# A cross attention's scores and values moved to small tiles of the array

## What is computed

```
def _L2_xattn_ref(q, k, v):            # h = 8, d = dv = 16, Tq = Tk = 256
    qh, kh, vh = (z.reshape(B, h, d, T) for z in (q, k, v))
    qn = _l2norm(qh, axis=-2)
    kn = _l2norm(kh, axis=-2)
    qk = 5.0 * jnp.einsum('bhdq,bhdk->bhqk', qn, kn)
    sm = jax.nn.softmax(qk, axis=-1)
    out = jnp.einsum('bhqk,bhdk->bhdq', sm, vh)
    return out.reshape(B, Dv, Tq)
...
x = x + jnp.tanh(g_xattn[2]) * _L2_xattn_ref(_layernorm(x, axis=-1), ctx_2048, ctx_2048)
```

## Time and profile before

| | us |
|---|---|
| median of 3 runs | 1113.99 |
| lowest, highest | 1108.63, 1115.76 |
| span of the profiled execution | 1103.1 |
| TensorE, its loads busy | 982.7, 646.4 |
| VectorE, ScalarE, GpSimd busy | 703.1, 468.2, 354.8 |
| mean granted TensorE clock | 0.941 |

### The profile page before, as it was taken

The page is one execution under the profiler, slowest core; times in us unless marked ns, Lnnn a source line. Parts: engine busy times, 40 slices in busy tenths (PEclk is TensorE's granted clock), DMA queues, the critical chain, the costliest instruction groups (busy, mean ns, idle before and its releaser), DMA issues.

```text
span 1103.1 us, 18620 instructions
## 1 busy us (share of the span) xinstructions
PE 982.7 (89%) x6482; PEld 646.4 (59%) x6482; DVE 703.1 (64%) x1490; ACT 468.2 (42%) x779; POOL 354.8 (32%) x362
## 2 busy tenths in 40 slices
PE   7888989999977887877777989999989999989997
PEld 4466664435655444444453569998479575854443
DVE  5887754434798999999968781112411250289998
ACT  3343322100269999999953443332113436410000
POOL 4142130000464666666634112210410547410002
PEclk9898888999987999999988999997989999799999
DMA  9100020000000000000000051003631415100001
GB/s 274 25 1 1 1 88 4 1 0 1 1 1 1 2 1 0 0 0 0 0 27 1 1 167 36 1 1 114 149 115 49 141 46 159 52 1 0 0 0 38
DMA packets 54276, 41.30 MB, mean 37 GB/s; under 512 B 17569, under 2 KB 52028, under 8 KB 54220
## 3 DMA queue, kind: packets, MB, share of 16 engines
q1 hardware_dynamic: 52684, 36.36, 11.9%
q0 software_dynamic: 1536, 4.20, 1.2%
HBM read 33.20 MB, written 7.34 MB: 37 GB/s over the span
## 4 chain that ended last, share of the span: by engine, by line
PE 68%; DVE 16%; issue 9%; ACT 4%; DVEq 2%; DMA 1%; POOL 0%; SPq 0%; ACTq 0%; POOLq 0%
PE psum L442 6%; PE psum L949 6%; PE psum L1381 5%; PE psum L1402 5%; PE psum L940 5%; DVE xn L2007 3%; PE psum L479 3%; PE psum L1506 3%; PE psum L592 2%; PE psum L608 2%; PE psum L1220 2%; PE psum L422 2%; PE psum L955 2%; PE psum L446 2%; DVE am L1102 2%
## 5 line engine op out<-in xcount | busy, mean ns | idle before, releaser
L1040 POOL TENSOR_SCALAR arena<-arena 128x1024 f16<-128x1024 f32 x128 | 133.7, 1044 | 94.4 <-ACT arena L1014 91.4
L1102 DVE TENSOR_REDUCE am<-psum 128x1024 f32 (+1 forms) x128 | 155.0, 1212 | 8.7 <-PE psum L940 8.6
L1014 ACT ACTIVATE arena<-psum,am 128x1024 f32<-128x1024 f32 x128 | 143.0, 1125 | 10.3 <-DVE am L1102 8.1
L949 PEld LDWEIGHTS psum<-identh,arena 128*128 128x128 f16 x1024 | 63.1, 100 | 94.3 <-issue 61.2
L949 PE MATMUL psum<-identh,arena 128*128 128x128 f16 x1024 | 82.0, 225 | 37.2 <-DVE xn L1107 36.3
L1949 PE MATMUL psum<-arena,cT 128*128 x512 | 110.9, 379 | 3.3 <-DVE xn L2007 2.8
L316 POOL TENSOR_TENSOR rstd<-ve,neg_half 128x1 f32<-128x1 f32 x64 | 39.0, 613 | 207.6 <-DVE ve L306 207.3
L2007 DVE SCALAR_TENSOR_TENSOR xn<-psum,small,xn 128x256 f32<-128x256 f32 x248 | 102.2, 478 | 4.9 <-DVE xn L2007 2.2
L940 PE MATMUL psum<-arena 96*128 96x512 bf16 x256 | 78.8, 392 | 11.6 <-ACT arena L1014 8.8
L1949 PEld LDWEIGHTS psum<-arena,cT 128*128 128x128 f16 x512 | 49.9, 98 | 63.8 <-DVE xn L2007 4.0
L1007 ACT ACTIVATE arena<-psum,m 128x1024 bf16<-128x1024 f16 x64 | 71.7, 1121 | 2.4 <-PE psum L949 2.4
(11 more groups left out here) (338 smaller groups left out, 1876.5 us busy)
## 6 DMA issues: line engine op xcount, KB each, us to landing
hT<-in_L_ffn_expert_masks SPq DMA_DIRECT2D x32, 256.0 KB, 2.9
arena<-in_L_ffn_w_gate SPq DMA_DIRECT2D x2, 1408.0 KB
arena<-in_L_ffn_w_up SPq DMA_DIRECT2D x2, 1408.0 KB
arena<-in_L_ffn_w_down SPq DMA_DIRECT2D x2, 1408.0 KB
moe_in<-xT SPq DMA_DIRECT2D x2, 1024.0 KB, 6.9
hT<-moe_in SPq DMA_DIRECT2D x4, 512.0 KB, 6.2
moe_out<-arena SPq DMA_DIRECT2D x16, 128.0 KB, 1.7
weights<-in_L_ffn_w SPq DMA_DIRECT2D x2, 640.0 KB, 6.0
```

The source lines that it names most:

```text
L949: mm = pe.transpose(bank[:, k * P:(k + 1) * P], Y1[:, hm % 2, k * P:(k + 1) * P], identh)
L1014: act.activation(PE1[:, h % 2, :], scores, ACT.Exp, bias=am[:, bass.ds(n, 1)], accum_out=qs[:, bass.ds(n, 1)]).then_inc(sig("p1_ready"), 1)
L1040: pool.tensor_scalar(Y1[:, n % 2, :], PE1[:, n % 2, :], 255.0, 1024.0, ALU.mult, ALU.add)\
L1102: dve.tensor_reduce(am[:, bass.ds(n, 1)], psum[:, 2 * SCORES[h]:2 * SCORES[h] + 2, :], AX.XY, ALU.max, negate=True)\
```

## The change

Both kinds of matmul move to tiles of a part of the array.

- **Scores.** Four groups g of 32 partitions hold two heads each. `masked_keys` makes two copies of the keys instead of eight, by the parity of the head (`par`), 128x512 in one product, all eight batches in tiles of their own. A score matmul contracts over 32 rows: `keys[rows, k, 128 keys]` as weights, `xn[rows, b, :]` streamed, for g = 0 to 3 in turn, each group into its own bank. One unit u is one parity k of one batch, so 16 units of 8 score matmuls.
- **Exponentials.** ScalarE takes a pair of banks in one activation of 1024 columns. Three pairs of banks (0 to 5) go round; four slots of exponentials.
- **Values.** The weights are now the values: for each head 32 columns (`VP`), 16 of them zero, those of the other parity; the exponentials are streamed, 256 columns. Four groups write the four 32-partition parts of one bank's first half. Four more matmuls of the same kind with ones in place of values (`ones2`) write the sums to the other half. So 16 matmuls a unit, and the outputs come out with tokens on the partitions; the transposes go.
- **Additions.** VectorE takes the reciprocal of all 128x256 sums, multiplies output, gate and reciprocal, and adds to X. Banks 6 and 7 alternate by batch; TensorE waits on `o2_read` before it writes one again, and once more at the end of the stage and ahead of the shared expert.
- **GpSimd.** Clears `VP` and `ones2` and fills them in `values2_pool`, makes the first four batches' keys there, and the other four once the norms' squares are read, since they lie in `sq2`.

```diff
-        PT2 = a.tile([4, DC, 2, D])
+        PT2 = a.tile([4, 2, DC, D])
...
-        cA = a.tile([DC, NB, H2, D2 + 1])
-        KM = a.tile([2, H2, D])
+        VP = a.tile([DC, NB, H2, 2 * D2])
+        ones2 = a.tile([2, 2 * D2])
+        KM = a.tile([NB // 2, 2, D])
+        KM_late = sq2.rearrange("p (b k) d -> p b k d", k=2)
...
-        STEPS2 = NB * H2 // 2
-        LAG_V2, LAG_B2 = 2, 3
+        STEPS2 = NB * 2
+        PAIRS2, SLOTS2 = 3, 4
+        def pair_banks(p):
+            return 2 * (p % PAIRS2)
+        def out2_bank(b):
+            bank = psum[:, 6 + (b + ids["out2_first"]) % 2, :]
+            return bank[:, 0:D], bank[:, D:2 * D]
...
         def masked_keys(pool, b):
-            if b >= 2:
-                pool.wait_ge(ring_a.full, ids["s2", 4 * (b - 2) + 3])
-            pool.tensor_tensor(KM[:, b % 2, :, :], bc(cx[:, b, :].unsqueeze(1), [P, H2, D]),
-                               bc(mask8.unsqueeze(2), [P, H2, D]), ALU.mult).then_inc(sig("km_ready"), 1)
+            pool.tensor_tensor(keys_of_pair(b), bc(cx[:, b, :].unsqueeze(1), [P, 2, D]),
+                               bc(par.unsqueeze(2), [P, 2, D]), ALU.mult).then_inc(sig("km_ready"), 1)
...
+            pool.memset(ones2, 0.0).then_inc(sig("vp_ready"), 1)
+            pool.memset(VP, 0.0).then_inc(sig("vp_ready"), 1)
...
         def xa2_pe(pe):
             norms_pe(pe, "q2", sq2)
...
+            def scores(u):
+                b, k = divmod(u, 2)
+                if k == 0:
+                    pe.wait_ge(sig("km_ready"), b + 1)
+                    pe.wait_ge(sig("q2_ready"), b + 1)
+                if 2 * u + 1 >= PAIRS2:
+                    pe.wait_ge(sig("p2_ready"), 2 * u + 2 - PAIRS2)
+                for kc in range(DC):
+                    for g in range(4):
+                        rows = slice(32 * g, 32 * g + 32)
+                        bank = psum[:, pair_banks(2 * u + g // 2) + g % 2, :]
+                        mm = pe.matmul(bank[:, kc * D:(kc + 1) * D], keys_of_pair(b)[rows, k, kc * P:(kc + 1) * P],
+                                       xn[rows, b, :], start=True, stop=True)
+                        if kc == DC - 1:
+                            mm.then_inc(sig(f"s2_pair{g // 2}_full"), 1)
+            def values(u):
+                b, k = divmod(u, 2)
+                out, total = out2_bank(b)
+                if k == 0 and b >= 2:
+                    pe.wait_ge(sig("o2_read"), b - 1)
+                pe.wait_ge(sig("p2_ready"), 2 * u + 2)
+                for kc in range(DC):
+                    first, last = k == 0 and kc == 0, k == 1 and kc == DC - 1
+                    for g in range(4):
+                        p = PT2[:, (2 * u + g // 2) % SLOTS2, g % 2, kc, :]
+                        pe.matmul(out[32 * g:32 * g + 32, :], VP[:, kc, b, 2 * g + k, :], p,
+                                  start=first, stop=last, skip_group_check=True)
+                    for g in range(4):
+                        p = PT2[:, (2 * u + g // 2) % SLOTS2, g % 2, kc, :]
+                        mm = pe.matmul(total[32 * g:32 * g + 32, :], ones2[:, k, :], p,
+                                       start=False, stop=last, skip_group_check=True)
+                        if kc == DC - 1:
+                            mm.then_inc(sig("v2_done"), 1)
+            for u in range(STEPS2 + 1):
+                if u < STEPS2:
+                    scores(u)
+                if u >= 1:
+                    values(u - 1)
+            pe.wait_ge(sig("o2_read"), NB - 1)
...
+            for p in range(2 * STEPS2):
+                u = p // 2
+                act.wait_ge(sig(f"s2_pair{p % 2}_full"), 2 * (u + 1))
+                if u >= 2:
+                    act.wait_ge(sig("v2_done"), 4 * (u - 1))
+                at = pair_banks(p)
+                act.activation(PT2[:, p % SLOTS2, :, :, :].rearrange("p g c q -> p (g c q)"),
+                               psum[:, at:at + 2, :].rearrange("p g n -> p (g n)"), ACT.Exp, scale=ALPHA)\
+                   .then_inc(sig("p2_ready"), 1)
...
+                dve.wait_ge(sig("v2_done"), 8 * (b + 1))
+                step(dve.reciprocal(share, total))
+                step.wait()
+                dve.scalar_tensor_tensor(share, out, gate(4), share, ALU.mult, ALU.mult).then_inc(sig("o2_read"), 1)
+                dve.wait_ge(sig("o2_read"), b + 1)
+                dve.tensor_tensor(X[:, b, :], X[:, b, :], share, ALU.add).then_inc(sig("x2_added"), 1)
...
+            pe.wait_ge(sig("o2_read"), NB)
             pe.wait_ge(sig("shared_loaded"), 16 * 4)
```

More of the change, by code:

```diff
@@ L1370, in xa2_pe @@
             norms_pe(pe, "q2", sq2)
[L1371 to L1384, removed]
-                if m >= 0 and m % 4 == 3:
-                    b = m // 4
-                    pe.wait_ge(ring_v.evacuated, ids["o2", b])
-                    bank = ring_v.claim(pe)
-                    for qc in range(DC):
-                        mm = pe.transpose(bank[:, qc * P:(qc + 1) * P], out2[:, b, qc * P:(qc + 1) * P], identf)
-                    ring_v.fill(mm)
-                m = n - LAG_V2
-                if 0 <= m < STEPS2:
-                    pe.wait_ge(ring_a.evacuated, ids["s2", m])
-                    b, g = divmod(m, H2 // 2)
-                    if g == 0:
-                        bank_o = ring_v.claim(pe)
-                    for qc in range(DC):
-                        for j in range(2):
-                            at = (qc * H2 + 2 * g + j) * (D2 + 1)
-                            for kc in range(DC):
-                                mm = pe.matmul(bank_o[:, at:at + D2 + 1], PT2[:, m % 4, kc, j, qc * P:(qc + 1) * P],
-                                               cA[:, kc, b, 2 * g + j, :], start=(kc == 0), stop=(kc == DC - 1))
-                    if g == H2 // 2 - 1:
-                        ids["o2", b] = ring_v.fill(mm)
-                    else:
-                        mm.then_inc(sig("values2"), 1)
@@ new lines, in xa2_pe @@
+            pe.wait_ge(sig("vp_ready"), N_VP)
+            pe.wait_ge(ring_a.evacuated, ids["q2", 3])
+            pe.wait_ge(ring_v.evacuated, ring_v.filled)
+            ids["out2_first"] = ring_v.filled % 2
+            def scores(u):
[13 more added lines that the diff above has]
+                            mm.then_inc(sig(f"s2_pair{g // 2}_full"), 1)
@@ L1414, in xa2_act @@
                 norms_act(act, i, inv2)
-            for n in range(STEPS2):
-                for kc in range(DC):
-                    bank = ring_a.take(act)
-                    if n >= 4 and kc == 0:
-                        b, g = divmod(n - 4, H2 // 2)
-                        if g == H2 // 2 - 1:
-                            act.wait_ge(ring_v.full, ids["o2", b])
-                        else:
-                            act.wait_ge(sig("values2"), 3 * b + g + 1)
-                    ring_a.release(act.activation(PT2[:, n % 4, kc, :, :].rearrange("p h q -> p (h q)"), bank, ACT.Exp, scale=ALPHA))
-        def xa2_pool(pool):
-            for b in range(NB + 4):
-                if 2 <= b < NB:
-                    masked_keys(pool, b)
-                if b >= 4:
-                    rstd_pool(pool, 5, b - 4)
+            for p in range(2 * STEPS2):
[7 more added lines that the diff above has]
+                   .then_inc(sig("p2_ready"), 1)
+        def xa2_pool(pool):
+            pool.wait_ge(ring_a.full, ids["q2", 3])
+            for b in range(NB // 2, NB):
+                masked_keys(pool, b)
+            for b in range(NB):
+                rstd_pool(pool, 5, b)
         def xa2_dve(dve, step):
```

29 lines of the change are left out of this document (14 added, 15 removed).

## The result

| | us | ratio to before, 95% interval |
|---|---|---|
| before, 4 runs | 1112.93 (1108.63 to 1115.76) | |
| after, 4 runs | 1043.51 (1042.11 to 1047.55) | 0.937 [0.934, 0.941] |
| predicted | 1100 (1062 to 1152) | |

The change takes 69 us off where 14 were forecast.

The account below looks back on a forecast made before the run. TensorE's stream was taken to bound the stage: 16 units of 6.05 us (96.8) plus 1.3, 1.7, 1.0 and 0.8 gave 101.6 against 115.7, so -14.1 us from 1113.99: 1100 us, range 1062 to 1152.

Parts of the forecast that it names:

- Overlap of tiles: TensorE's scores and values: neighbouring tiles overlap by one fp32 half only, 0.219 us for each matmul of the program.
- Loads: TensorE's weight loads: hidden for scores (1.75 us a unit), 0.028 us exposed for each value matmul (3.95 us a unit).
- the rival: Four tiles abreast in scores and values: unit 3.86 us, bound by 16 score loads; -49 us, 1065 us; chance 0.20.
- Switch: TensorE changing between row tiles and column tiles, twice a unit: 0.35 us for the pair.
- Fill: Stage start: scores of unit 1 wait for pair 0's exponential, with no values to lie over it; +1.3 us.
- cold start: First scores of the stage run partly at the half clock, 1.2 GHz, as before the change; +1.7 us.
- late products: Four late key products on GpSimd beside VectorE's first queries: between 0 and 2.4 us, taken as +1.0.
- Tail: After the last value: reciprocal over 128x256, two further pieces and handovers take 2.8 us against 2.0; +0.8 us.
- What lies beside: ScalarE (2.0 us a unit), VectorE (about 4 us a batch) and GpSimd's preparation stay hidden; clock gain taken as 0.
- The span: Whole kernel: median of runs 1113.99 us against profiled span 1103.1; the 10.9 us between them kept unchanged.
- columns serial: Value matmuls on column tiles take turns: 7.01 us a unit, +35 us, 1149 us; chance 0.17.
- no overlap at all: No tile overlaps in scores or values: unit 10.86 us, stage 178.6, +63 us, 1177 us; chance 0.11.

Follow-up runs that it names:

- The orders of four, six and eight passes: Changed kernel with four, six or eight passes of one column tile in a row before the next tile's: 0.942, 0.955 and 0.981 of before.
- one half: Kernel after with tiled scores but the old values (exponentials as weights, 17 columns streamed, outputs transposed) and two pairs of score banks: 1.014 of before.

## Why the prediction was wrong

- **Overlap of tiles: the step that failed.** "Then the second half of one tile and the first half of the next run side by side, and nothing more." Every row of before had its matmuls start in order, but every row was one tile: order within a tile and order of the stream look the same there. The orders of four, six and eight passes show that the column tiles keep only the first, with a queue of four; the row tiles start in fours with two passes of a tile in a row. The Trainium skill, "TensorE: Matmul & The Clock Gate", Part 3, has matmuls "pc-monotone in start AND end"; the trace of eight in a row disagrees, where a pass that stands ninth in the program starts 0.21 us ahead of the sixth. Four matmul records take one round of 0.216 us where I had two streaming times. Worth 1.75 - 0.86 = 0.89 us of scores and 3.50 - 1.73 = 1.77 of values a unit, so 2.66 of the 3.11 that the unit was too long.
- **Loads.** I charged 0.028 us for each value load, the other 0.45 a unit, and the rival 0.110 for each score load, 1.76 a unit. They run four at a time and hide: but for the first behind a switch, score rounds are 0.216 with loads of 128 columns in them. That is why the rival's 3.86 a unit was too long as well, 2.94 being measured. The same Part 3 of the Trainium skill's page, in its list of what overlaps, lets a load overlap only where the row group differs; the loads of the column tiles, all on the same rows, start in fours under matmuls in flight too.
- **Switch, 0.35 a unit.** Measured 0.34 to 0.35, and 0.33 and 0.41 with one side on the whole array. Right.
- **Fill 1.3, cold start 1.7, late products 1.0.** 16 units of 2.94 are 47.0, so 6.7 us are these instead of 4.0: 2.9 for the first two intervals (3.20 and 5.59) at clock 0.50, 1.4 for the unit of 4.35 that waits for VectorE, 2.3 for the values of the last unit, which nothing overlays. The late products made one pass of VectorE (L1345, at 634.7) 0.85 us longer, but the query behind it was ready at 638.0 and its scores started at 643.7; what was late is the first addition, behind all the queries.
- **Tail +0.8.** From the last reciprocal to the router's logits (L348) 5.36 became 6.12 us: +0.8. Right. From there to the first down product of an expert (L1514) it is 0.9 less; the clock was 0.62 there against 0.50 in the earlier trace rows, and I had taken 0.
- **What lies beside.** ScalarE at 1021 ns an exponential holds, and VectorE stays under TensorE, with 32.4 busy of 44.8 us. Ahead of the stage I counted GpSimd's changed preparation as hidden in its idle 32 us. It was (clearing took 3.5 us, not 10), but what it did to VectorE while it ran wasn't: the row with 2.87 us had shown that, and I used it at one place only. Worth 5.8 us (4.9 in the stretch above, 0.9 behind it).
- **The span.** I took 10.9 us of each run to lie around the span. It is 1.8 (1116.39 and 1114.6): the profiled execution was a quick one. The difference that I predicted isn't touched by it.

Sum by the traces, from L928 to the first down product of an expert (L1514): stage -62.0, ahead -5.8, tail and clock -0.2; that stretch fell from 476.3 to 408.4, 67.9. The medians say 69.4. Against the forecast's -14.1: the unit brings 16 x 3.11 = 49.8 more, fill, start and waits take back 2.7, ahead and clock bring 6.7, and that is the 53.8 between them.

The rivals: columns serial (0.302 us as the point that decides) and no overlap at all are ruled out: the 16 value matmuls of a unit take 1.86 us, 0.116 each.

## What to carry to other kernels

Small tiles on a quarter of the array run four abreast even where each matmul is two passes, as long as no column tile has more than four passes in a row in the stream (row tiles were tried with two): interleave the tiles, and count rounds, not records. When a trace lacks the case that you price, ask what its rows can't tell apart (here order in a tile and order in the stream), and give the untested one more than 0.20. A half of such a change may lose where the whole gains: here the granted clock stayed at 0.50 with one half and rose to 1.00 with both. And where an engine gets four times faster, look who is next: here VectorE's order of work and then ScalarE's exponentials.

## What the runs showed of the hardware

- Passes of four 32-row or four 32-column tiles start 6 to 7 ns apart in fp32. A column tile takes up to four passes into its queue, and a fifth holds up all tiles (unit 2.98, 4.31 and 5.60 us for four, six and eight in a row).
- At granted clock 1.00 a round of 256 columns is 0.216 us in fp32 and 0.11 in fp16, and a matmul is two passes in fp32 and one in fp16. A pair of switches between row and column tiles costs 0.34 to 0.35.
- TensorE busy for 147 of 150 us stayed at granted clock 0.50 with 32-row scores and 17-column values. With 128-row scores in the same places it rose.
- A GpSimd product over 2048 columns stretches a VectorE pass from 0.69 to 3.54 us, and clearing 4096 columns on GpSimd two short ones from 0.93 to 4.18.
